# Attention stage of a graph network: two shared PSUM banks handed over one at a time

## The reference

```python
rad = relu(edge_attr @ W1 + b1) @ W2          # for keys (W1k, W2k) and values (W1v, W2v)
g   = edge_sh @ Wang.T
k,v = x_src * g @ Wlin * rad                  # x_src = node_attr[src], 128 wide
alpha  = einsum('ehq,qk,ehk->eh', q[dst], Wdot, k)
attn   = softmax of alpha over the edges of each dst
out    = segment_sum(attn[..., None] * v, dst) # then @ Wout
```

## Time and profile before

| | |
|---|---|
| median of 3 runs | 5324.31 us (5315.24 to 5349.9) |
| profiled execution | 5315.98 us, its span 5314.2 us |
| mean granted TensorE clock | 0.89 of full speed |
| busy, share of the span | TensorE 79%, its weight loads 65%, VectorE 57%, ScalarE 36%, GpSimd 36% |
| DMA | 944 MB moved, mean 178 GB/s |

### The profile page before, as it was taken

The page is one execution under the profiler, slowest core; times in us unless marked ns, Lnnn a source line. Parts: engine busy times, 40 slices in busy tenths (PEclk is TensorE's granted clock), DMA queues, the critical chain, the costliest instruction groups (busy, mean ns, idle before and its releaser), DMA issues. The chain is left out here.

```text
span 5314.2 us, 73086 instructions
## 1 busy us (share of the span) xinstructions
PE 4215.5 (79%) x26543; PEld 3463.0 (65%) x26543; DVE 3027.4 (57%) x4129; ACT 1934.3 (36%) x2481; POOL 1919.0 (36%) x2002
## 2 busy tenths in 40 slices
PE   4658999999999945777787878788877878777842
PEld 4657999999999843655565656566665656555632
DVE  8985444544443334656666655656655656566634
ACT  5655666666565412222222222222222222222213
POOL 5640000000000055444554554545554554455352
PEclk8879999999999957889989888988888888899965
DMA  7988999999995434444555544555554555455433
GB/s 169 190 186 283 296 294 295 292 299 291 298 295 192 132 88 129 142 144 143 147 152 148 148 142 137 149 148 151 148 145 143 147 149 148 146 148 149 141 115 48
DMA packets 1012831, 944.01 MB, mean 178 GB/s; under 512 B 705677, under 2 KB 811929, under 8 KB 1012339
## 3 DMA queue, kind: packets, MB, share of 16 engines
q1 hardware_dynamic: 952099, 814.71, 52.1%
q0 software_dynamic: 60368, 124.52, 9.8%
HBM read 648.66 MB, written 289.97 MB: 177 GB/s over the span
## 5 line engine op out<-in xcount | busy, mean ns | idle before, releaser
L2313 POOL DMA_INDIRECT feats_hops<-x_table,src_s x1616 | 1547.1, 957 | 1499.7 <-PE e_turn_ps L2421 1046.8
L1286 PE MATMUL acc<-t_wide,scaled 128*128 128x448 f32 x6860 | 1409.2, 367 | 24.3 <-DVE t_wide L1380 24.3
L1286 PEld LDWEIGHTS acc<-t_wide,scaled 128*128 128x128 f32 x6860 | 1284.8, 188 | 129.1 <-DVE scaled L1398 24.7
L1321 ACT CAST t_wide<-t_ring 128x1568 fp32r<-128x1568 uint8 x490 | 737.7, 1506 | 565.0 <-PE acc L1286 542.6
L1380 DVE CAST t_wide<-t_ring 128x1568 fp32r<-128x1568 uint8 x490 | 478.3, 976 | 733.6 <-PE acc L1286 714.0
L2349 PE MATMUL e_turn_ps<-e_weighted,e_spot 128*128 128x128 f32 x3232 | 506.8, 322 | 283.0 <-issue 271.4
L2349 PEld LDWEIGHTS e_turn_ps<-e_weighted,e_spot 128*128 128x128 f32 x3232 | 469.3, 231 | 322.6 <-issue 311.3
L2482 ACT COPY e_out_rows<-e_turn_ps 128x1024 f32<-128x1024 f32 x202 | 204.5, 1012 | 917.6 <-remote 604.9
L1809 POOL MEMSET l_eps<- 128x1 f32 x1 | 0.1, 104 | 1452.6 <-POOLq L1498 1452.6
L2542 DVE TENSOR_TENSOR feats_hops<-e_ring_ps,e_x_t 128x1024 f32<-128x1024 f32 x202 | 247.2, 1224 | 474.2 <-remote 327.7
L2400 PE MATMUL e_ring_ps<-e_wlin_v,e_x_gv 128*128 128x128 f32 x3232 | 457.5, 294 | 48.3 <-issue 43.3
(11 more groups left out here) (272 smaller groups left out, 5080.9 us busy)
## 6 DMA issues: line engine op xcount, KB each, us to landing
t_ring<-adjacency_bytes SPq DMA_DIRECT2D x490, 512.0 KB, 5.7
sums_table<-e_out_rows SPq DMA_DIRECT2D x202, 576.0 KB
q_first<-hop_zeros_q SPq DMA_DIRECT2D x101, 512.0 KB, 5.9
e_sh<-parts_sh SPq DMA_DIRECT2D x404, 128.0 KB
e_ea<-parts_ea SPq DMA_DIRECT2D x404, 128.0 KB
e_q_rows<-q_first SPq DMA_DIRECT2D x404, 128.0 KB
e_same<-same_row SPq DMA_DIRECT2D x404, 128.0 KB
adjacency_bytes<-lists_staged SPq DMA_DIRECT2D x196, 256.0 KB
```

The costliest lines, as they stand in the source:

```text
L1286: mm = nc.tensor.matmul(acc[c][:, 0:n], U[p][:, b, :], wide[m % WIDE_RING][:, lo:lo + n], start=(b == 0 and p == 0), stop=(b == NB - 1 and ...
L1321: nc.scalar.copy(into, of).then_inc(wide_act, 1)
L2313: nc.gpsimd.indirect_dma_start(x_rows[i % XR][:, g * GT + t, :], None, x1_table, bass.IndirectOffsetOnAxis(ap=src_ix[:, at:at + 1], axis=0 ...
```

## The change

Each of the two banks of `turn_ps` gets its own hand-over. `turn_x`, `spread_out` and `hidden` wait for bank 0, fill it and count, then wait for bank 1, fill it and count. ScalarE copies sums and x as two instructions of 512 columns, one for each bank, each with its own wait and count; the two hidden copies, two instructions before as well, now each have their own wait and count. All counts of `p_xt`, `p_seg`, `p_hid`, `a_xt`, `a_out` and `a_hid` go up by two a pair, and the waits on them on SyncE, GpSimd and VectorE are doubled: these still wait for both halves. `turn_weights` still waits for both banks and counts once.

```diff
             def spread_out(j, i):
                 pe.wait_ge(v_weighted, j + 1)
-                pe.wait_ge(a_hid, min(i + 2, N))
-                if j >= 1:
-                    pe.wait_ge(a_out, j)
                 if not on(i + 1) and chain_at(i - 2) is not None:
                     pe.wait_ge(a_wt, 3 * chain_at(i - 2) + 3)
-                for k in range(K):
-                    mm = nc.tensor.matmul(turn_ps[:, k // GT, k % GT * P:(k % GT + 1) * P], spot[j % 2][:, k, :],
-                                          weighted[j % 2][:, k, :], start=True, stop=True)
-                mm.then_inc(p_seg, 1)
+                for h in range(2):
+                    pe.wait_ge(a_hid, 2 * min(i + 1, N - 1) + h + 1)
+                    if j >= 1:
+                        pe.wait_ge(a_out, 2 * (j - 1) + h + 1)
+                    for t in range(GT):
+                        mm = nc.tensor.matmul(turn_ps[:, h, t * P:(t + 1) * P], spot[j % 2][:, h * GT + t, :],
+                                              weighted[j % 2][:, h * GT + t, :], start=True, stop=True)
+                    mm.then_inc(p_seg, 1)
 
             def turn_weights(n, i):
                 pe.wait_ge(a_exp, n + 1)
                 pe.wait_ge(v_lsum, n + 1)
                 if on(i + 1):
-                    pe.wait_ge(a_xt, i + 2)
+                    pe.wait_ge(a_xt, 2 * (i + 2))
                 else:
-                    pe.wait_ge(a_hid, N)
+                    pe.wait_ge(a_hid, 2 * N)
                     if i - LAG - 1 >= 0:
-                        pe.wait_ge(a_out, i - LAG)
+                        pe.wait_ge(a_out, 2 * (i - LAG))
                 if n >= 1:
                     pe.wait_ge(a_wt, 3 * n)
                 for c, src in enumerate((weight, most, lsum)):
@@ -2385,7 +2386,7 @@
             def keys_and_radial(i):
                 s = i % 2
                 pe.wait_ge(v_gk, i + 1)
-                pe.wait_ge(a_hid, i + 1)
+                pe.wait_ge(a_hid, 2 * i + 1)
                 bank = ring_bank(5 * i + 4)
                 nc.tensor.matmul(bank[:, 1, :], w2k[:], hid_k[s][:], start=True, stop=True).then_inc(p_rk, 1)
                 for g in range(2):
@@ -2413,25 +2414,25 @@
 
             def turn_x(r, i):
                 pe.wait_ge(x_got[r % XR], 16 * K * (r // XR + 1))
-                if r >= 1:
-                    pe.wait_ge(a_hid, r)
-                if i - LAG - 1 >= 0:
-                    pe.wait_ge(a_out, i - LAG)
-                for k in range(K):
-                    tr = nc.tensor.transpose(turn_ps[:, k // GT, k % GT * P:(k % GT + 1) * P], x_rows[r % XR][:, k, :],
-                                             ident[:])
-                tr.then_inc(p_xt, 1)
+                for h in range(2):
+                    if r >= 1:
+                        pe.wait_ge(a_hid, 2 * (r - 1) + h + 1)
+                    if i - LAG - 1 >= 0:
+                        pe.wait_ge(a_out, 2 * (i - LAG - 1) + h + 1)
+                    for t in range(GT):
+                        tr = nc.tensor.transpose(turn_ps[:, h, t * P:(t + 1) * P], x_rows[r % XR][:, h * GT + t, :],
+                                                 ident[:])
+                    tr.then_inc(p_xt, 1)
 
             def hidden(r, i):
                 s = r % 2
                 pe.wait_ge(ea_in[s], 32 * (r // 2 + 1))
-                pe.wait_ge(a_xt, r + 1)
-                if chain_at(i - 2) is not None:
-                    pe.wait_ge(a_wt, 3 * chain_at(i - 2) + 3)
                 for n in range(2):
-                    mm = nc.tensor.matmul(turn_ps[:, n, :], stack[:, n * D:(n + 1) * D], ea[s][:],
-                                          start=True, stop=True)
-                mm.then_inc(p_hid, 1)
+                    pe.wait_ge(a_xt, 2 * r + n + 1)
+                    if chain_at(i - 2) is not None:
+                        pe.wait_ge(a_wt, 3 * chain_at(i - 2) + 2 + n)
+                    nc.tensor.matmul(turn_ps[:, n, :], stack[:, n * D:(n + 1) * D], ea[s][:],
+                                     start=True, stop=True).then_inc(p_hid, 1)
 
             def turn_q(r):
                 s = r % 2
@@ -2476,11 +2477,12 @@
         def _(act):
             def keep_rows(j):
                 n, p = divmod(j, BATCH)
-                act.wait_ge(p_seg, j + 1)
                 if j >= 2:
                     act.wait_ge(stored[j % 2], 16 * (j // 2))
-                nc.scalar.copy(out_rows[j % 2][:, :, 0:D].rearrange("e (g t) d -> e g t d", g=2),
-                               turn_ps[:].rearrange("e g (t d) -> e g t d", d=D)).then_inc(a_out, 1)
+                for h in range(2):
+                    act.wait_ge(p_seg, 2 * j + h + 1)
+                    nc.scalar.copy(out_rows[j % 2][:, h * GT:(h + 1) * GT, 0:D],
+                                   turn_ps[:, h, :].rearrange("e (t d) -> e t d", d=D)).then_inc(a_out, 1)
                 act.wait_ge(a_wt, 3 * n + 3)
                 nc.scalar.copy(out_rows[j % 2][:, :, D:ROW],
                                ml_t[n % 2][:, p * K * 2 * H:(p + 1) * K * 2 * H].rearrange("e (k c) -> e k c", k=K)
@@ -2499,16 +2501,18 @@
                                    ).then_inc(a_wt, 1)
 
             def keep_x(r):
-                act.wait_ge(p_xt, r + 1)
                 if r >= 2:
                     act.wait_ge(v_gv, r - 1)
-                nc.scalar.copy(x_t[r % 2][:], turn_ps[:]).then_inc(a_xt, 1)
+                for h in range(2):
+                    act.wait_ge(p_xt, 2 * r + h + 1)
+                    nc.scalar.copy(x_t[r % 2][:, h, :], turn_ps[:, h, :]).then_inc(a_xt, 1)
 
             def keep_hidden(r):
-                act.wait_ge(p_hid, r + 1)
+                act.wait_ge(p_hid, 2 * r + 1)
                 if r >= 2:
                     act.wait_ge(p_rk, r - 1)
-                nc.scalar.activation(hid_k[r % 2][:], turn_ps[:, 0, :], ACT.Relu, bias=b1[0][:, 0:1])
+                nc.scalar.activation(hid_k[r % 2][:], turn_ps[:, 0, :], ACT.Relu, bias=b1[0][:, 0:1]).then_inc(a_hid, 1)
+                act.wait_ge(p_hid, 2 * r + 2)
                 if r >= VR:
                     act.wait_ge(p_rv, r - VR + 1)
                 nc.scalar.activation(hid_v[:, r % VR, :], turn_ps[:, 1, :], ACT.Relu,
@@ -2536,7 +2540,7 @@
```

More of the change, by code:

```diff
@@ L2258, in load @@
                 if i >= 2:
-                    sp.wait_ge(p_hid, i - 1)
+                    sp.wait_ge(p_hid, 2 * (i - 1))
                 for g in range(2):
@@ L2283, in store @@
             def store(j):
-                sp.wait_ge(a_out, j + 1)
+                sp.wait_ge(a_out, 2 * j + 2)
                 sp.wait_ge(a_rows, j + 1)
@@ L2308, in _ @@
                 if i >= XR:
-                    pool.wait_ge(p_xt, i - XR + 1)
+                    pool.wait_ge(p_xt, 2 * (i - XR + 1))
                 for g in range(2):
@@ L2538, in gate @@
                 dve.wait_ge(p_gk, i + 1)
-                dve.wait_ge(a_xt, i + 1)
+                dve.wait_ge(a_xt, 2 * i + 2)
                 if i >= 2:
@@ L2552, in find_spots @@
                 if j >= 2:
-                    dve.wait_ge(p_seg, j - 1)
+                    dve.wait_ge(p_seg, 2 * (j - 1))
                 dve.wait_ge(v_spot, 2 * j + 1)
```

## The result

The changed kernel takes 5056.6 us (median of 4 runs, 5041.39 to 5069.92) against 5322.7 us before (4 runs, 5315.24 to 5349.9): a ratio of 0.949 [0.947, 0.952], 5.1% faster. I had forecast 5237 us, with 5150 as the lowest, so the direction was right and the size was far off. The gain also hangs on a condition that the experiments brought out: in some groups of runs the kernel before takes 4342 us, and there the change is worth about 1% (0.991 in e12, which has one more wait in it).

A forecast was written before the change was run, and what follows sets the result against it. The prediction took the attention loop to be bound by TensorE signals held during gathers, released some 11.7 us after the first. It summed 5316.0 - 54 - 33 = 5229 us, forecast 5237 against the 5324 median, range 5150 to 5345.

The forecast's parts named there:

- What bounds the kernel: Attention loop: TensorE's signals are held while gathers run, the last released some 11.7 us after the first gather starts.
- The rival that took the hold for something else's doing: TensorE's signals are held by something other than gathers: no change, 5324 us; chance 0.24 shared with signals paying for themselves.
- Halves of the sums' copy and the turning: ScalarE's sums copy and TensorE's turning cut in two: 0.42 us saved in each of 129 iterations, 54 us.
- (a): Both halves of the sums released together after the gathers: first gather after 2.23 us instead of 2.49, gain 0.26 us.
- (b): First half of the sums released at least 0.59 us earlier: 1.64 us to the first gather, gain 0.85 us.
- Sums after the first hidden copy: Where the hidden signal is late, sums start 0.58 us sooner: 0.45 us taken for each of 73 iterations, 33 us.
- the number of late iterations: Iterations whose turning waits for no sums copy, the hidden signal being late: taken as 73 of 202.
- fewer late iterations: Rival: half hand-over keeps TensorE awake, turning 25 of 73 late iterations into the first kind, 58 us more; chance 0.10.
- The cost terms: Copying in pieces costs ScalarE 0.26 us per tile, 53 us if uncovered; added TensorE waits at most 0.15 us, while idle.
- Each signal pays for itself: Rival: each held TensorE signal costs a 1.42 us step; 5290 to 5356 us, chance 0.24 shared with no gathers' doing.
- The second hidden signal is held: Rival: second hidden matmul's signal waits until the gathers end, 2.3 us more per iteration hit, slower; chance 0.14.
- What would show it: Signs: shorter turning wait, 1.6 to 2.2 us from second copy to gather, sums 0.1 us after first hidden copy, constant 11.7.

The follow-up runs named there:

- e12: Whole change, plus SyncE's loads held back until the x rows are copied, against the kernel before at about 4342 us: 4298.9 us, ratio 0.991.
- e8: Kernel before with one gather of eight for each pair, the other tiles holding old data: 4338.9 us in one run, against 5326 us before.
- e6: Only the hidden layers handed over by halves, sums and x rows whole, against the kernel before at about 5325 us: 5286.4 us, ratio 0.993.
- e1: Only the hidden layers handed over by halves, sums and x rows whole, against the kernel before at 4343 us: 4313.2 us, ratio 0.993.
- e7: Only sums and x rows handed over by halves, hidden layers whole, against the kernel before at about 5325 us: 5049.2 us, ratio 0.947.
- e3: Kernel before with only doubled signal counts from TensorE, waits and copies as before, where the kernel before took 4343 us: 4342.8 us, ratio 1.000.

## Why the prediction was right in direction and wrong in size

- **What bounds the kernel: right.** Where the turning waits for the copy, the release came 11.72 us after the first gather before, and 11.61 after where both halves come together; the path from release over copy and turning to the next gather is shorter. That the hold needs the gathers was argued then and is shown by e8, for the condition of these runs. The rival that took the hold for something else's doing falls. The rule of the Trainium skill (SBUF — State Buffer, "SBUF: two separate sides") that DMA and compute don't slow each other is stated of the ports of SBUF; carried over to TensorE's signals, as that rival did, it doesn't agree with the runs: 5326 us with eight gathers, 4339 with one.
- **Halves of the sums' copy and the turning: both bounds occur, the size taken was too small.** (a) was 2.23 us from release to gather, 2.12 in the iteration shown (the pair of copies takes 1.07 us, not 1.28); (b) was 1.64, and 1.63 in the other. But the iterations in which the turning waits became 14.46 - 13.72 = 0.74 us shorter, not 0.42. A part of it is the slow turning after an idle stretch (1.94 us in rows 3), which the prediction named and left out of its sum: 29 of the 104 such iterations before had it and took 14.99 us each, the other 75 took 14.26.
- **Sums after the first hidden copy: right where it applies, but it hardly applied.** After the change the sums start 0.1 us behind the first hidden copy in all 18 iterations in which that copy is over 1 us late, as forecast. Yet these are few now. e6 holds this edit by itself: it gives 40 us where 33 were taken, and its 56 iterations without the turning's wait take 16.13 us for 16.84. How much of the 40 us is from this edit is open, as the same kernel gains 30 us without the hold (e1), where no iteration is late.
- **The failed step: the number of late iterations was held fixed at 73.** Both terms of the sum were multiplied by counts read before the change (129 and 73), as if the edit could not alter them. Measured, the iterations without the turning's wait fell from 58 of 162 to 13 of 180, which is from 72 to 15 of 202. With the times of before, 14.46 and 16.84 us, that alone is worth 0.68 us an iteration, 0.68 x 202 = 137 us. The remaining 0.81 us, some 163 us, is the shorter iteration of each kind, where the two terms together had 87. (The sum, 300, is over the 275 of the stage, whose last iterations have no gathers.) The rival "fewer late iterations" named the step, with a chance of 0.10, 25 of 73, and the half hand-over as the cause; it was 57 of 72, and the part with the sums and x did it (e7 against e6), not that of the hidden layers.
- **The cost terms** held: ScalarE's 38 us of extra copying (53 forecast) is covered as far as the time shows, and no row shows a cost of the added waits.
- **The other rivals.** "Each signal pays for itself" falls: a gap of 1.4 us between the copies of the halves is real (3104.51, 3105.93, and in 20 of 180 iterations), but where the turning waits and the copies are over 0.8 us apart, the second starts 11.52 us after the first gather on average, against 12.10 where they are together. So the first comes earlier, not the second later. "The second hidden signal is held" falls as a cost: the two hidden copies start over 1 us apart in 12 of 181 iterations, at most 2.1 us. e3 shows that more signals cost nothing without the hold; with it that was not tried.
- **What would show it.** Right were the 1.6 to 2.2 us from the second copy to the gather (1.73 on average where the turning waits), the 0.1 us from the first hidden copy to the sums, and the constant 11.7. The turning's mean wait for the sums' copy fell as forecast if taken for one wait (1.86 to 281.0 / 186 = 1.51 us), but rose if taken for one iteration (1.2 to 1.5), because the iterations without that wait, the long ones, went away.

What stays open: why the edit of sums and x lets the *hidden* signal through in time, when the hidden hand-over itself does not; which of the two it takes, and whether it is the copies in halves or only the added signals; and what puts a group of runs into one condition or the other.

## What to carry to other kernels

When a loop shows two kinds of iteration, don't multiply a saving by the counts of before: ask what decides which kind comes next, and price the case that the slow kind goes altogether, since it is worth more than the edit's own fraction of a microsecond. An edit can pay in a stage of the loop that it does not touch, so run each part alone. And compare only within a group of runs: here a part was worth 5% or 0.3% by a condition that the kernel's own time before reveals.

## What the runs showed of the hardware that was not expected

- The same kernel took 4342 us or 5325 us, on the same chips at different times. The traces agree up to the first writes to `turn_ps`, at 1971.8 us in both. Some 937 us of the difference lie in the attention loop (its last sums end at 5091.5 us with the hold and at 4155.0 in e3, with the same order of work without it), and 37 us in the layer behind it (220 for 183), which has gathers too. With the longer time TensorE's signals reach the other engines up to some 11.7 us after the first gather, while TensorE's records show the matmuls long over. With the shorter, the hidden copy started 0.8 us or less after the start of its matmuls in every iteration of e3, with all eight gathers.
- With that hold, taking out seven of eight gathers gave back 987 us (5326 to 4339, one execution), though GpSimd is busy with gathers for only half of the stage.
- Held signals mostly come out together, and else in steps. In 180 iterations after, the second of the two copies of sums starts 0.5 us behind the first in 139, back to back, 1.4 us behind in 20, 0.7 in 7, 2.8 in 7, and between 1.6 and 4.2 in the other 7.
- Two ScalarE copies of 512 columns of PSUM take 1.07 us back to back, where one of 1024 takes 1.01: cutting such a copy costs 0.06 us of time from start to end, not the 0.27 that I had from the hidden copies.
